# Feed-forward bias of a graph network: copied by ScalarE into the banks ahead of a 32-row product, in place of a product of ones on TensorE

## The reference, cut to what matters

```
a = ...                                  # attention, zero where no edge arrives
x = layernorm(h + a @ Wo, ln1_g, ln1_b)  # first norm: gain and bias
f = relu(x @ W1 + b1) @ W2 + b2          # W1 512 x 32, W2 32 x 512
return layernorm(x + f, ln2_g, ln2_b)
```

## Time and profile before

| | us |
|---|---|
| median of 3 runs | 2785.97 (2780.97 to 2790.19) |
| the profiled execution, its own time | 2781.79 |
| its span in the profile | 2780.0 |
| TensorE busy in the span | 2290.1 |
| VectorE busy | 1806.6 |
| GpSimd busy | 1135.8 |
| ScalarE busy | 1008.9 |

### The profile page before, as it was taken

The page is one execution under the profiler, slowest core; times in us unless marked ns, Lnnn a source line. Parts: engine busy times, 40 slices in busy tenths (PEclk is TensorE's granted clock), DMA queues, the critical chain, the costliest instruction groups (busy, mean ns, idle before and its releaser), DMA issues.

```text
span 2780.0 us, 28864 instructions
## 1 busy us (share of the span) xinstructions
PE 2290.1 (82%) x9582; PEld 1197.5 (43%) x9582; DVE 1806.6 (65%) x3856; ACT 1008.9 (36%) x1735; POOL 1135.8 (41%) x869
## 2 busy tenths in 40 slices
PE   8999999999999689996076766739998898389786
PEld 4455555555555345453031211214444553254465
DVE  7999888888878861445753433544567658557753
ACT  2354545454555432210432322321121132265553
POOL 2766654455675724301645665620210201233222
PEclk9999999999999889998587988869999697599898
DMA  7333443333343435325744645670210202222221
GB/s 245 99 103 105 118 121 120 104 118 108 108 111 104 129 95 167 104 76 165 206 139 134 175 131 155 153 222 10 67 48 27 73 1 74 75 71 69 57 57 53
DMA packets 214547, 298.62 MB, mean 107 GB/s; under 512 B 100006, under 2 KB 100501, under 8 KB 213018
## 3 DMA queue, kind: packets, MB, share of 16 engines
q1 hardware_dynamic: 108186, 213.98, 25.7%
q0 software_dynamic: 106240, 83.12, 12.1%
HBM read 171.66 MB, written 160.65 MB: 120 GB/s over the span
## 4 chain that ended last, share of the span: by engine, by line
PE 56%; DVE 20%; issue 7%; POOL 6%; DMA 5%; ACT 5%; SPq 1%; POOLq 0%; DVEq 0%; ACTq 0%
PE bank L2031 8%; PE bank L320 8%; PE bank L1010 7%; PE bank L304 5%; POOL arena L1624 4%; PE bank L2627 3%; PE bank L296 3%; PE bank L990 2%; PE bank L311 2%; DMA arena<-y_table,ids 2%; DVE st L642 2%; POOL arena L1102 2%; PE bank L312 2%; PE bank L2510 2%; DMA x_table<-arena 2%
## 5 line engine op out<-in xcount | busy, mean ns | idle before, releaser
L1102 POOL DMA_INDIRECT arena<-x_table,idd x120 | 152.0, 1267 | 648.2 <-DVE arena L2297 157.1
L1678 PE MATMUL bank<-arena 125*125 125x512 f32 x360 | 207.5, 709 | 108.6 <-DMA arena<-y_table,ids 103.7
L2031 PE MATMUL bank<-arena 128*125 128x512 f32 x640 | 293.7, 614 | 1.4 <-DVE Md L2251 0.7
L304 PE MATMUL bank<-arena 128*125 128x512 f32 x640 | 285.2, 599 | 8.6 <-DMA ident<-ident_in 8.6
L1624 POOL DMA_INDIRECT arena<-y_table,ids x180 | 229.6, 1276 | 153.1 <-DMA y_table<-arena 101.0
L320 PE MATMUL bank<-arena 128*125 128x512 f32 x640 | 278.5, 593 | 2.1 <-ACT arena L517 1.8
L1852 DVE SCALAR_TENSOR_TENSOR arena<-arena,v,bank 125x512 f32<-125x512 f32 x180 | 134.3, 746 | 188.1 <-PE bank L1678 180.0
L811 POOL TENSOR_TENSOR arena<-arena,rowv 125x512 f32<-125x512 f32 x80 | 99.5, 1278 | 315.4 <-DVE arena L725 201.7
L1018 ACT ACTIVATE arena<-bank 128x500 f32<-128x500 f32 (+1 forms) x210 | 114.6, 589 | 279.3 <-PE bank L962 145.4
L1010 PE MATMUL bank<-arena 128*125 128x512 f32 x480 | 208.8, 593 | 0.0
L1729 ACT ACTIVATE bank<-arena 125x512 f32<-125x512 f32 x180 | 107.6, 600 | 267.5 <-DVE arena L1852 262.4
(11 more groups left out here) (404 smaller groups left out, 4417.4 us busy)
## 6 DMA issues: line engine op xcount, KB each, us to landing
y_table<-arena SPq DMA_DIRECT2D x36, 896.0 KB
p_table<-arena SPq DMA_DIRECT2D x25, 896.0 KB
z_table<-arena SPq DMA_DIRECT2D x25, 896.0 KB
x_table<-arena SPq DMA_DIRECT2D x25, 896.0 KB
arena<-x_cols SPq DMA_DIRECT2D x20, 1000.0 KB, 6.4
arena<-x SPq DMA_DIRECT2D x20, 896.0 KB
out<-arena SPq DMA_DIRECT2D x20, 896.0 KB
x_by_src<-arena SPq DMA_DIRECT2D x5, 896.0 KB
```

Of the source, the lines that this page charges most:

```text
L304: i = nc.tensor.matmul(b[0:P, :], xT[:, k, j * P:(j + 1) * P], W1r[:, k, :], start=k == 0, stop=k == KC - 1)
L1102: nc.gpsimd.indirect_dma_start(out=dst, out_offset=None, in_=table, in_offset=bass.IndirectOffsetOnAxis(ap=idx, axis=0), bounds_check=limi ...
L1678: nc.tensor.matmul(bank[t % RING1][0:P, :], Ss[:, t, :], V1[:, t, :], start=False, stop=True, skip_group_check=True).then_inc(P_sum, 1)
L2031: i = nc.tensor.matmul(b[0:P, :], fT[:, k, j * P:(j + 1) * P], W[:, k, :], start=k == 0, stop=k == KC - 1)
```

## The change

- TensorE loses the four products of 2 rows in each of 20 steps. Its four products of 32 rows no longer start the bank (`start=False`): they add to what is there, and wait for a new semaphore `ffn_rows`.
- ScalarE gains four copies in each of these steps, right behind the rows of `T`: the bias row, held in all 125 partitions as `ffn_b`, goes into each bank of `b_f`, once `NR_sb` says that the bank is empty.
- DVE gains one addition of 125x512 (`ln1_b` + `b2`) at the end of step 1, and loses the fill of `ones4`.
- SyncE gains two loads of a row to 125 partitions ahead of the second group's rows, and loses four small loads of `w_ffn`.

```
@@ sp_second_loads
+            for dst, r in ((ffn_b, R_LN1B), (ffn_b2, R_L2B2)):
+                sp.dma_start(dst, rows[r].partition_broadcast(P)).then_inc(s_rows, 16)
             sp_rows(sp, 1, 1)
...
-            for j in range(TG):
-                sp.dma_start(w2x4[32 * j:32 * j + 2, 1, :], w_ffn[0:2, D:2 * D]).then_inc(s_w2, 16)
@@ pe_step
                 bs = [r_bank("b_f", j) for j in range(TG)]
-                for j in range(TG):
-                    nc.tensor.matmul(bs[j][0:P, :], f1T[32 * j:32 * j + 32, :], w2x4[32 * j:32 * j + 32, 0, :],
-                                     start=True, stop=False)
-                for j in range(TG):
-                    nc.tensor.matmul(bs[j][0:P, :], ones4[32 * j:32 * j + 2, :], w2x4[32 * j:32 * j + 2, 1, :],
-                                     start=False, stop=True).then_inc(NR_ps, 1)
+                pe.wait_ge(ffn_rows, 4 * nL + 4)
+                for j in range(TG):
+                    nc.tensor.matmul(bs[j][0:P, :], f1T[32 * j:32 * j + 32, :], w2x4[32 * j:32 * j + 32, :],
+                                     start=False, stop=True, skip_group_check=True).then_inc(NR_ps, 1)
@@ act_step
                     nc.scalar.activation(T[1 - par][:, j, :], Z[1 - par][:, j, :], ACT.Identity,
                                          scale=rs[:, 0, j:j + 1], bias=nb[:, 0, j:j + 1]).then_inc(A["t"], 1)
+            if has(s, "L"):
+                if isinstance(s, int) and s == LAG["L"]:
+                    act.wait_ge(wp_rdy, 2)
+                for j in range(TG):
+                    u = st_.count("b_f", j)
+                    act.wait_ge(NR_sb, u - (len(RB) - 1))
+                    nc.scalar.activation(st_.bank("b_f", j)[0:P, :], ffn_b, ACT.Identity).then_inc(ffn_rows, 1)
@@ vector, end of step 1
+                        nc.vector.tensor_tensor(ffn_b, ffn_b, ffn_b2, ALU.add).then_inc(wp_rdy, 1)
```

More of the change, by code:

```diff
@@ L104, in gnn_kernel @@
         kd = at(23848, [2, 2 * ET], P)
-        w2x4 = at(35499, [2, D])
-        WM0, maps, ones4 = at(36523, [128]), at(36651, [M_END, 128]), at(37675, [P])
+        w2x4, ffn_b = at(35499, [D]), at(36011, [D], P)
+        ffn_b2 = at(23928, [D], P)
+        WM0, maps = at(36523, [128]), at(36651, [M_END, 128])
         wleft, wrep = at(24576, [4, 128]), at(25088, [2, P])
@@ L119, in gnn_kernel @@
         wm_rdy, wp_rdy = sem("weights_multiplied"), sem("weight_columns_spread")
+        ffn_rows = sem("ffn_bias_rows")
         A = {k: sem("A_" + k) for k in
@@ L261, in sp_second_loads @@
             sp.dma_start(key_table.rearrange("(h l) q -> h l q", l=LO), tab).then_inc(tab_put, 16)
-            for dst, src in ((wleft, w_left), (w2x4[:, 0, :], w_ffn[:, 0:D])):
+            for dst, src in ((wleft, w_left), (w2x4, w_ffn)):
                 sp.dma_start(dst, src).then_inc(s_w2, 16)
-            for j in range(TG):
-                sp.dma_start(w2x4[32 * j:32 * j + 2, 1, :], w_ffn[0:2, D:2 * D]).then_inc(s_w2, 16)
         def sp_out(sp, n):
@@ L344, in pe_step @@
                 if isinstance(s, int) and s == 1:
-                    pe.wait_ge(s_w2, 16 * 7)
+                    pe.wait_ge(s_w2, 16 * 3)
                 pe.wait_ge(A["t"], 4 * s)
@@ L394, in pe_step @@
                 pe.wait_ge(NT_sb, st_.count("w_m", 1))
-                pe.wait_ge(wp_rdy, 2)
+                pe.wait_ge(wp_rdy, 1)
                 for m in range(2):
@@ L1868, in dve_L1 @@
             dve.wait_ge(w2_in, 16 * 2)
-            nc.vector.tensor_tensor(row(R_FFN), row(R_FFN), J1[:, 0, :], ALU.add).then_inc(ffn_row, 1)
+            nc.vector.tensor_tensor(row(R_FFN), row(R_FFN), J1[:, 0, :], ALU.add).then_inc(ffn_rows, 1)
             with dve.Fori(2, ITERS - 1) as i:
@@ L1929, in mask_slot @@
             return 3 * (j - 1) + k
-        w2_in, q_rdy, e_rdy, f_rdy, ft_rdy = (sem(k) for k in "w2_in q_ready e_ready fc_ready ft_ready".split())
+        w2_in, e_rdy, f_rdy, ft_rdy = (sem(k) for k in "w2_in e_ready fc_ready ft_ready".split())
         ex_in, ex_rdy, at_rdy, x3_put, bd_rdy = (sem(k) for k in "ex_in ex_ready attn_ready x3_put bd_ready".split())
-        ffn_row = q_rdy
         A_L1 = 256
@@ L1957, in sp_L2 @@
             sp.dma_start(RD[:, :, :], RSd.rearrange("(t p) q -> p t q", p=P)).then_inc(rec_back, 16)
-            sp.wait_ge(s_w2, 16 * 9)
+            sp.wait_ge(s_w2, 16 * 5)
             sp.dma_start(C3[:, 0:M_NDC, :], maps_d[:, 0:M_NDC * 128]).then_inc(w2_in, 16)
@@ L2050, in pe_L2 @@
             pe.wait_ge(s_w1, 64)
-            pe.wait_ge(ffn_row, 1)
+            pe.wait_ge(ffn_rows, 4 * NG + 1)
             pe.wait_ge(*x2_s[0].full(16 * TG))
@@ L2983, in _ @@
         def _(dve):
-            nc.vector.memset(ones4, 1.0).then_inc(wp_rdy, 1)
             nc.vector.memset(dups[:, :, 0:1], 0.0)
@@ L2989, in _ @@
             dve.wait_ge(s_w1, 48)
-            dve.wait_ge(wp_rdy, 1)
             nc.vector.tensor_copy(wrep[:, 0, :], colv[:, C_BG2:C_BG2 + 1].broadcast_to([128, P]))
@@ L3001, in step @@
                         dve.wait_ge(NT_sb, st_.count("w_g", 1))
-                        dve.wait_ge(s_rows, 16)
-                        dve.wait_ge(s_w2, 16 * 7)
+                        dve.wait_ge(s_rows, 16 * 3)
+                        dve.wait_ge(s_w2, 16 * 3)
+                        nc.vector.tensor_tensor(ffn_b, ffn_b, ffn_b2, ALU.add).then_inc(wp_rdy, 1)
                         nc.vector.tensor_copy(maps[:, M_ND1, :], wcol(W_ND1, 128))
@@ L3023, in step @@
                 if isinstance(s, int) and s == LAG["B"]:
-                    pool.wait_ge(s_rows, 16)
+                    pool.wait_ge(s_rows, 16 * 3)
                 pool_step(pool, st_, s, par)
@@ L3081 @@
     w32[:, V_F2:V_END] = np.tile(np.concatenate([f2, s2, a["L3_gnn_W_f1"]], axis=1), (4, 1))
-    w_ffn = np.concatenate([np.tile(a["L2_gnn_W2"], (4, 1)), np.zeros((128, D), f32)], axis=1)
-    w_ffn[0, D:], w_ffn[1, D:] = a["L2_gnn_ln1_b"], a["L2_gnn_b2"]
+    w_ffn = np.tile(a["L2_gnn_W2"], (4, 1))
     g2T = a["L3_gnn_W_g2"][:, 0:128].T
```

## The result

The changed kernel takes 2793.71 us (median of 20 runs, 2783.64 to 2808.24), the kernel before 2784.73 us beside it (20 runs, 2775.44 to 2795.06). The ratio is 1.0034, 95% interval 1.0022 to 1.0047: 9.4 us slower (6.1 to 13.1), where the prediction had 5.3. So I compare stretches of the traces, and not their spans.

The account below looks back on a forecast made before the run. TensorE was taken to bound steps 3, 9 to 13 and nearly 17 and 18, POOL and DVE steps 4 to 8. Terms summed to +3.6 us, plus 1.7 for a clock loss: +5.3, median 2791.3 us, range 2782 to 2799.

Parts of the forecast that it names:

- Step 2, +8.7: `b_f` waits for copies behind a late `T`; `a_o1` 7.2 us late plus 1.5 for half clock, between 6.5 and 10.5.
- step 3's own wait for the copies: In step 3 the copies end 0.7 us after `b_f`'s old start; less 0.96 saved, -0.3 us.
- The removal, 0.96 us: Dropping the four 2-row products takes 0.96 us from TensorE in each of 20 steps, bounds 0.86 and 1.06.
- Steps 9 to 13: TensorE's time is the time there: 5 x 0.96 saved, less 0.5 us of occasional waits, -4.2 us (-4.8 to 0).
- The first rival: POOL and DVE bound steps 9 to 13, so those five steps give nothing: +4.2, 2795.5 us; chance 0.14.
- Steps 4 to 8, 0, and 1.7 for one clock loss: `b_f` is off the POOL-DVE circle, so nothing gained; longer idle stretches at the gate cost one more clock loss, +1.7 us.
- the second rival: The clock falls in most longer stretches of steps 4 to 8 and 16: +4 to +6, about 2796 us; chance 0.14.
- The third rival: In steps 4 to 8 DVE's squares finish before POOL's L798, saving 3.7 us a step, 2776.5 with four; chance 0.09.
- Steps 14 to 18: Step 14 gains 0.4 us, steps 15 and 16 nothing, steps 17 and 18 together 1.9; step 15's copies miss by 0.6.
- Step 20, +2.1: In the drain the copies end after `b_f`'s old start, so DVE's addition starts at 926.2 instead of 924.10: +2.1 us.
- step 21, -0.4: Step 21 has no `T`; one copy of 0.6 us is added and 0.96 saved: -0.4 us.
- The copies' price, 2.0 us behind `T`: On ScalarE, the four copies put the last bias in its bank 2.0 us after `T` ends, bounds 1.9 and 2.4.

Follow-up runs that it names:

- e12: The changed kernel run and profiled a second time, nothing altered: ratio 1.0031 to the kernel before (1.0012 to 1.0051).
- e4: The kernel before with one wait added: in step 2 TensorE's `b_f` waits for the rows of `T`. Ratio 1.0044 to the kernel before.
- e7: The changed kernel with step 2's copies moved to the end of step 1, ahead of the root, and GpSimd adding `ln1_b` + `b2`: ratio 1.0027 to the kernel before.
- e9: The changed kernel with step 2's copies early, ahead of the root, and 2-row products of zeros in steps 4 to 7: ratio 0.9996 to the kernel before.
- e11: The changed kernel with two 2-row products of zeros right ahead of the gate's own, behind the idle stretch, in steps 4 to 7: ratio 1.0069 to the kernel before.
- e1: The changed kernel with step 2's copies ahead of `T` but still behind the root, and GpSimd adding the two rows: ratio 1.0038 to the kernel before.
- e13: e9 run and profiled a second time, nothing altered: ratio 0.9985 to the kernel before (0.9967 to 1.0002).
- e5: The changed kernel with four 2-row products added again behind the 32-row ones, copies and waits kept: ratio 1.0051 to the kernel before.
- e8: The changed kernel with four 2-row products of zeros behind the 32-row ones in steps 4 to 7 alone: ratio 1.0023 to the kernel before.
- e3: The kernel before without the four 2-row products, the bias left out of the node phase and nothing in their place: ratio 1.0008 to the kernel before.

## Why the prediction was right, and where not

The direction and the range (2782 to 2799) held; the forecast was 4 us short. The 0.34% lies just beyond the 0.3% up to which I had called it no change (0.62); slower than that had 0.30. By the two profiles of the changed kernel, steps 2 and 3 cost 1.7 us more than forecast, steps 4 to 8 2.7 more, steps 9 to 18 0.9 more, and the drain 1.3 less.

- **Step 2, +8.7.** The mechanism was right, the size not: `a_o1` was 10.6 us late, step 3's `b_f` 11.4 (e12: 10.5). `b_f` started at 98.64 instead of the 97.8 of the forecast; `T` itself came 0.7 later, as it did by 0.9 in e4, which has none of the change's other edits. Of the 11.4 us, 0.8 are step 3's own wait for the copies, which the forecast had as 0.7. The half clock cost 2.2 us up to `a_o1` (1.26 on `a_p2`, 0.94 on `b_f`) and not 1.5. e4 has the cost alone, e7 and e9 are without it.
- **The removal, 0.96 us.** It is worth 0.86, the lower bound: 45.41 became 44.55. I had taken the distance of the starts in one step, and not what the period of a step loses. Steps 9 to 13 gave 4.1 us (forecast 4.2), with no wait for copies in any. The first rival, that POOL and DVE bound these steps, is false.
- **Steps 4 to 8, 0, and 1.7 for one clock loss.** This is the step that failed. I wrote that nothing is gained there, which is true, and that the longer stretch costs one more loss. It costs one in nearly every step: with DVE's holds, +7 us in the mean of the five profiles without the products (-1.4 to +10.2 in single ones; +4.4 in the two of the changed kernel). That was the second rival, to which I gave 0.14, because four of five stretches of 2.5 us had kept the clock; those rows say nothing of 3.4. The row that I named for it, 4.62 us with the clock lost, weighed more. The Trainium skill, "TensorE: Matmul & The Clock Gate", section "HAM oscillation — how this bites in real kernels", describes this: a wait between tiles that is long enough, and comes back in every tile, takes the clock every time. The traces agree in 21 of 23 stretches; 3.20 us (e12, step 7) and 3.35 us (e11, step 8) kept it.
- **DVE held by POOL.** I had looked for it in the squares and in L761. It came at L793 in step 4 (5.95 us; in e1 too). The third rival, squares that get through ahead of POOL, is seen in step 8 of e9, e12 and e13 (45.6 us instead of 48.1). Both happen, in both directions, so that one profile of these steps is worth little.
- **Steps 14 to 18.** Step 17 gave 0.87, step 16 0.8 that I had not counted, 14 and 18 nothing, and step 15 took 0.3: -1.5 for the forecast's -2.3. That step 15 would miss by 0.6 was right: `b_f` idled 0.70 there.
- **Step 20, +2.1, step 21, -0.4.** `b_f` idled 4.17 us instead of 1.05. From step 19's `b_f` to the end of the node phase, the nine profiles with copies there have a mean of 138.7 us (133.8 to 141.7), the five without 136.1 (132.9 to 139.5). That fits +1.7, and doesn't prove it.
- **The copies' price, 2.0 us behind `T`.** 2.14 for four, 2.19 from `T` to `b_f`. Right. ScalarE's own time costs nothing (e5).

The account over the two profiles of the changed kernel, as means against the one of before: step 2 +11.0, step 3 -0.9, steps 4 to 8 +4.4, steps 9 to 13 -4.0, steps 14 to 18 -1.6, the drain +0.4. Together +9.3, and the times say 9.4 (6.1 to 13.1). That they meet so closely is luck: the two profiles end their node phases 9 us apart, and there is one of before.

What stays open: how the 9.4 us split between the two costs in the mean of many runs, since e7 and e8 each gave back less than their traces show; what lengthens steps 14 to 18 in e1, e3, e4 and e5; and what decides in one execution which DVE instruction is held.

## What to carry to other kernels

Where TensorE already idles in each step on something else, work taken from it lengthens the idle stretch, and the clock that falls behind it can cost more than the work did (a loss of 1.6 us or more for 0.86 us of work): keep such work, or take it out only in the steps where TensorE has no idle time. A wait added for one engine has to be followed through every instruction ahead of it in the giving engine's queue, in the first and last steps too: step 2 alone cost more than steps 9 to 13 gave. And compare several profiles before reading 10 us out of a stretch where DVE and GpSimd meet.

## What the runs showed of the hardware

- The clock of TensorE behind an idle stretch is not a yes or no at one length: 2.3 to 2.5 us lost it in 11 of 38, 3.2 to 3.6 us in 21 of 23, in this place of this kernel. A loss made a step of 48.1 us 1.6 us longer where its window has a PEclk of 0.97, and about 3 where it has 0.93.
- A DVE instruction of 125x4 (0.16 us elsewhere) took 5.95 us, until four GpSimd instructions back to back had all ended; being small did not save it. The Trainium skill, "GPSIMD Engine Reference", section "Specifications", says that GpSimd shares its SBUF interfaces with VectorE, in contention with DVE instructions of two SBUF inputs, which this one has. How long a hold lasts is read from the rows alone.
- Four 2-row products added or removed are worth 0.86 us together at full clock (45.41 to 44.55 us a step), some 0.21 us each, though each has only 2 rows to multiply.
- A ScalarE copy of 125x512 into PSUM takes 578 ns (median of 80), four back to back 2.14 us, where four evacuations out of PSUM take 2.02.
